# Value output products 1 to 3 from rounded parts, their rests and batch 1's right-operand sums on GpSimd

## What is computed

```python
Q = (img_embed @ Wq).reshape(B, -1, H, D).transpose(0, 2, 1, 3)
K = (sent_embed @ Wk).reshape(B, -1, H, D).transpose(0, 2, 1, 3)
V = (sent_embed @ Wv).reshape(B, -1, H, D).transpose(0, 2, 1, 3)
score = jnp.einsum('bhqd,bhkd->bhqk', Q, K) / math.sqrt(D)
attn = jax.nn.softmax(jnp.where(mask, score, -jnp.inf), axis=-1)
ctx = jnp.einsum('bhqk,bhkd->bqhd', attn, V).reshape(B, -1, H * D)
out = ctx @ Wo + img_embed
return (out - mu) * jax.lax.rsqrt(var + EPS) * gamma + beta
```

## Time and profile before

| | |
|---|---|
| median of 3 runs | 354.56 us (354.5 to 354.85) |
| the profiled execution | 354.68 us, of which 352.9 us are the span |
| TensorE | busy 347.1 us, 98% of the span |
| VectorE | busy 285.6 us, 81% |
| ScalarE | busy 238.8 us, 68% |
| GpSimd | busy 201.1 us, 57% |

### The profile page before, as it was taken

The page is one execution under the profiler, slowest core; times in us unless marked ns, Lnnn a source line. Parts: engine busy times, 40 slices in busy tenths (PEclk is TensorE's granted clock), DMA queues, the critical chain, the costliest instruction groups (busy, mean ns, idle before and its releaser), DMA issues.

```text
span 352.9 us, 6849 instructions
## 1 busy us (share of the span) xinstructions
PE 347.1 (98%) x2272; PEld 323.5 (92%) x2272; DVE 285.6 (81%) x523; ACT 238.8 (68%) x790; POOL 201.1 (57%) x212
## 2 busy tenths in 40 slices
PE   9999999999999999999999999999999999999994
PEld 6999999999999999998899899889988998899884
DVE  2159999999866467898798888987987989889896
ACT  3267766545555669887886976977778769768560
POOL 0045654400004858689769688688696796884243
PEclk9999999999999999999999999999999999999998
DMA  7999758775645070053142341440532423413012
GB/s 235 425 418 321 275 227 336 286 255 211 220 158 190 0 285 15 4 178 120 61 172 68 119 151 55 156 150 33 179 105 75 158 72 131 149 46 105 32 50 101
DMA packets 19683, 55.81 MB, mean 158 GB/s; under 512 B 1728, under 2 KB 3264, under 8 KB 17728
## 3 DMA queue, kind: packets, MB, share of 16 engines
q1 hardware_dynamic: 18784, 54.38, 42.2%
q10 hardware_dynamic: 864, 1.00, 1.1%
HBM read 46.98 MB, written 8.39 MB: 157 GB/s over the span
## 4 chain that ended last, share of the span: by engine, by line
PE 98%; DVE 0%; DVEq 0%; issue 0%
PE pair L670 30%; PE pair L595 27%; PE pair L480 17%; PE pair L487 15%; PE pair L657 5%; PE pair L585 1%; PE pair L692 1%; PE pair L687 1%; DVE centred L1187 0%; DVEq L103 0%; DVE stats_last L1179 0%; DVE mean_var L1184 0%; DVE var_eps L1159 0%; PE pair L605 0%; DVE out_sb L1173 0%
## 5 line engine op out<-in xcount | busy, mean ns | idle before, releaser
L670 PE MATMUL pair<-vw_hi,pt_hi 128*128 128x512 f32 x155 | 62.3, 402 | 0.0
L670 PE MATMUL pair<-vw_hi,pt_lo 128*128 128x512 f32 x155 | 60.9, 393 | 0.0
L670 PE MATMUL pair<-vw_lo,pt_hi 128*128 128x512 f32 x155 | 60.6, 391 | 0.0
L1312 POOL TENSOR_TENSOR out_sb<-centred,beta_sb 128x512 f32<-128x512 f32 x30 | 38.8, 1294 | 29.2 <-ACT centred L864 29.1
L1363 POOL TENSOR_TENSOR w_proj_lo<-w_proj,w_proj_hi 128x768 fp32r<-128x768 f32 x14 | 25.7, 1859 | 39.1 <-ACT w_proj_hi L755 39.1
L819 ACT ACTIVATE prob<-c,neg_max 128x77 f32<-128x77 f32 x128 | 43.9, 346 | 0.0
L480 PE MATMUL pair<-kv_t,w_out_hi 128*128 128x308 f32 x160 | 42.0, 336 | 0.0
L1357 POOL TENSOR_TENSOR xo_lo<-x_sum,xo_hi 128x512 fp32r<-128x512 f32 x32 | 41.4, 1299 | 0.5 <-ACT xo_hi L843 0.5
L595 PE MATMUL pair<-a_hi,xo_hi 128*128 128x308 f32 x128 | 40.4, 316 | 0.0
L1332 POOL TENSOR_TENSOR x_sum<-xt_in 128x256 f32<-128x256 f32 x16 | 11.9, 745 | 47.6 <-DMA xt_in<-x_tiles 47.4
L595 PE MATMUL pair<-a_hi,xo_lo 128*128 128x308 f32 x128 | 38.9, 304 | 0.0
(11 more groups left out here) (121 smaller groups left out, 1021.1 us busy)
## 6 DMA issues: line engine op xcount, KB each, us to landing
w_out<-wo SPq DMA_DIRECT2D x8, 1024.0 KB, 4.8
xt_in<-x_tiles SPq DMA_DIRECT2D x16, 512.0 KB, 4.0
x_in<-x_rows SPq DMA_DIRECT2D x16, 512.0 KB, 4.8
out<-out_sb SPq DMA_DIRECT2D x31, 256.0 KB, 2.2
w_out<-wq_t SPq DMA_DIRECT2D x7, 1024.0 KB, 7.6
w_proj<-wv SPq DMA_DIRECT2D x8, 768.0 KB, 4.7
w_proj<-wk SPq DMA_DIRECT2D x6, 768.0 KB, 9.6
w_out<-wq_t SPq DMA_DIRECT2D x2, 512.0 KB, 8.1
```

The costliest lines, as they stand in the source:

```text
L670: mm = pe.matmul(ps_out[:, i % 2, 0:s.model], ps[:, j, :], v[:, b, j, :], start=(j == 0 and n == 0), stop=(j == s.key_t - 1 and n == len(p ...
L1312: pool.tensor_tensor(out_sb[i % OUT_RING][:, :], centred[i % 2][:, :], beta_sb[:, :], ALU.add)\
```

## The change

Value products 9, 10 and 11 are split too. Their six half rests are divided: GpSimd makes those of uses 9 and 10 and the second half of 11, VectorE the first half of 11. GpSimd also makes the ten steps of batch 1's right sums; batch 0's stay on VectorE. T_PARTS is ordered by batch, so batch 1's sums are rounded and subtracted later, up to use 13. The sums' buffers no longer lie in the `xt_in` tiles themselves but in new tensors of other scopes over reused space, and `kv_full1`, the second whole value of the start, has one of its own. `add_kv`, which summed the two parts of use 9's values for a whole product, goes. The sequence of TensorE's matmuls changes in products 9 to 11 alone.

```diff
-    SPLIT_VALUES = (H, *range(H + 4, USES - 1))
+    SPLIT_VALUES = range(H, USES - 1)
+    POOL_HALVES = ((H + 1, 0), (H + 1, 1), (H + 2, 0), (H + 2, 1), (H + 3, 1))
...
-    T_PARTS = [(n, b) for n in (T1, T2, T4, T3) for b in range(s.batches)]
+    T_PARTS = [(n, b) for b in range(s.batches) for n in (T1, T2, T4, T3)]
...
@@ tensor
-                        pe.wait_ge(dve_o_lo, 2 * split_before(u) + half + 1)
+                        if (u, half) in POOL_HALVES:
+                            pe.wait_ge(pool_o_lo, rests_before(u, half, True) + 1)
+                        else:
+                            pe.wait_ge(dve_o_lo, rests_before(u, half, False) + 1)
...
@@ scalar, in the loop over u
                 if u == H + 1:
-                    for part in T_PARTS[:4]:
-                        round_t(*part)
+                    round_t(T1, 0)
                 elif u == H + 2:
-                    for part in T_PARTS[4:6]:
-                        round_t(*part)
+                    round_t(T4, 0)
                 elif u == H + 3:
+                    round_t(T3, 0)
+                    round_t(T1, 1)
+                elif u == H + 4:
+                    round_t(T4, 1)
+                elif u == H + 5:
                     round_t(T3, 1)
...
                 if u + 1 < USES and not whole_out(u + 1):
                     round_w_out(u + 1)
+                if u == H + 1:
+                    round_t(T2, 0)
+                elif u == H + 3:
+                    round_t(T2, 1)
                 take_out_product(u, 1)
...
@@ vector, in the loop over u
-                if u == H:
-                    right_sum(T1, 0)
...
+                if u == H + 1:
+                    split_t(T1, 0)
+                    right_sum(T4)
+                elif u == H + 2:
+                    split_t(T4, 0)
+                elif u == H + 3:
+                    split_t(T3, 0)
+                    split_t(T1, 1)
+                elif u == H + 4:
+                    split_t(T4, 1)
+                elif u == H + 5:
+                    split_t(T3, 1)
                 if not whole_out(u):
                     add_out_product(u, 0)
+                if u == H:
+                    right_sum(T1)
+                elif u == H + 1:
+                    split_t(T2, 0)
...
                 if not whole_out(u):
                     add_out_product(u, 1)
                 if u == H:
-                    right_sum(T1, 1)
-                    right_sum(T2, 0)
-                    right_sum(T2, 1)
+                    right_sum(T2)
                 elif u == H + 1:
...
+                    right_sum(T3)
...
@@ gpsimd
+            def split_w_out(u):
+                for half in range(2):
+                    if (u, half) in POOL_HALVES:
+                        pool.wait_ge(act_o_hi, 2 * split_before(u) + half + 1)
+                        pool.tensor_tensor(half_cols(w_out_lo[u % W_RING], half), half_cols(w_out_sb[u % W_RING], half),
+                                           half_cols(w_out_hi[u % 2], half).bitcast(F32), ALU.subtract)\
+                            .then_inc(pool_o_lo, 1)
...
+            split_w_out(H + 1)
+            split_w_out(H + 2)
+            right_sum(T1)
+            split_w_out(H + 3)
+            right_sum(T2)
+            right_sum(T4)
+            right_sum(T3)
             block_sums(0)
```

More of the change, by code:

```diff
@@ L157, in build @@
         with ExitStack() as spare:
-            t_tmp4 = [spare.enter_context(nc.sbuf_tensor(f"t_tmp4_{b}", [P, KT, s.half], F32)) for b in range(s.batches)]
+            kv_full1 = spare.enter_context(nc.sbuf_tensor("kv_full1", [P, s.dim_t, s.toks], F32))
         w_out_hi1 = sb("w_out_hi1", [P, s.model_t, s.dim_t, P], F32R)
@@ L163, in build @@
         vw_lo = sb("vw_lo", [P, s.batches, s.key_t, s.model], F32R)
+        with ExitStack() as spare:
+            t_tmp_x = [spare.enter_context(nc.sbuf_tensor(f"t_tmp_x{b}", [P, KT, s.half], F32)) for b in range(s.batches)]
+            t_tmp_z0 = spare.enter_context(nc.sbuf_tensor("t_tmp_z0", [P, KT, s.half], F32))
         xt_in = [sb(f"xt_in{n}", [P, CHUNK, s.model]) for n in range(XT_RING)]
@@ L171, in build @@
         t_lo0 = sb("t_lo0", [P, 3, KT, s.half], F32R)
+        with ExitStack() as spare:
+            spare.enter_context(nc.sbuf_tensor("gap7", [P, T4, KT, s.half], F32))
+            t_tmp_z1 = spare.enter_context(nc.sbuf_tensor("t_tmp_z1", [P, KT, s.half], F32))
         t_hi1 = sb("t_hi1", [P, 3, KT, s.half], F32R)
@@ L316, in whole_out, with rests_before @@
             return u < FULL_OUT or (u >= H and u not in SPLIT_VALUES)
-        def summed_kv(u):
-            return whole_out(u) and not whole(u)
         def split_before(u):
             return sum(not whole_out(v) for v in range(u))
+        def rests_before(u, half, by_pool):
+            return sum(((v, n) in POOL_HALVES) == by_pool for v in range(u + 1) if not whole_out(v)
+                       for n in range(2) if (v, n) < (u, half))
         def summed_before(u):
@@ L352, in use_w_proj, with t_in @@
             return use(u - (W_RING if u % W_RING < 2 else 0), W_RING)
[L354 to L360, removed]
+        t_tmp = [[t_tmp_x[0][:, :, :], prob1[:, :].rearrange("p (k n) -> p k n", k=KT), t_tmp_z0[:, :, :]],
+                 [t_tmp_x[1][:, :, :], t_tmp3[:, :, :], t_tmp_z1[:, :, :]]]
+        T3_IN = (2, 0)
+        def t_in(n, b):
+            return t_tmp[b][{T1: 0, T2: 1, T4: 0, T3: T3_IN[b]}[n]]
         def right_steps(b):
             x, y, z = t_tmp[b]
+            last = t_tmp[b][T3_IN[b]]
             hi = [[right(a_hi, b, half, cols).bitcast(F32) for cols in range(2)] for half in range(2)]
@@ L376, in steps_of, with t_done @@
             return range(T_STEPS[n - 1] if n else 0, T_STEPS[n])
-        def t_done(n, b):
-            ahead = [part for part in T_PARTS if t_no[part] <= t_no[n, b]]
-            return sum(len(steps_of(m)) for m, _ in ahead)
+        def t_done(n):
+            return T_STEPS[n]
         def batch_of(p):
@@ L491, in wait_kv @@
             def wait_kv(u, half):
-                if summed_kv(u):
-                    pe.wait_ge(dve_kv_sum, 2 * sum(summed_kv(v) for v in range(u)) + half + 1)
-                elif whole_out(u):
+                if whole_out(u):
                     pe.wait_ge(act_kv_hi, 2 * u + half + 1)
@@ L993, in split_kv @@
                        .then_inc(dve_kv_lo, 1)
[L995 to L1000, removed]
             def take_out_product(u, half):
@@ L1216, in _ @@
                     split_w_out(u + 1)
+                if u == H + 3:
+                    split_t(T2, 1)
                 if not whole_out(u):
@@ L1358, in split_sums, with right_sum @@
                                    xo_hi[p % 2][:, blocks, :, :].bitcast(F32), ALU.subtract).then_inc(pool_xo_lo, 1)
+            def split_w_out(u):
+                for half in range(2):
+                    if (u, half) in POOL_HALVES:
+                        pool.wait_ge(act_o_hi, 2 * split_before(u) + half + 1)
+                        pool.tensor_tensor(half_cols(w_out_lo[u % W_RING], half), half_cols(w_out_sb[u % W_RING], half),
+                                           half_cols(w_out_hi[u % 2], half).bitcast(F32), ALU.subtract)\
+                            .then_inc(pool_o_lo, 1)
+            def right_sum(n):
+                if n == T1:
+                    pool.wait_ge(dve_a_lo, 2 * H)
+                    pool.wait_ge(dve_kv_lo, 2 * split_before(FROM_FULL))
+                elif n in (T4, T3):
+                    before = (T1 if n == T4 else T4, 1)
+                    pool.wait_ge(act_t_hi, t_no[before])
+                    pool.wait_ge(dve_t_lo, t_no[before])
+                for k in steps_of(n):
+                    to, x, y, op = t_steps[1][k]
+                    if k:
+                        pool.wait_ge(pool_t, k)
+                    pool.tensor_tensor(to, x, y, op).then_inc(pool_t, 1)
             for u in range(FULL_PROJ, FROM_FULL):
```

48 lines of the change are left out of this document (16 added, 32 removed).

## The result

The changed kernel takes 366.74 us (366.7 to 366.88), the kernel before in the same rounds 354.56 us (354.5 to 354.91): ratio 1.0341 (1.0326 to 1.0356), 12.2 us slower. The forecast was 366.7 us. The profiled execution has a span of 365.1 us against 352.9, so the span holds the whole difference.

What follows compares the result with a forecast made beforehand. The prediction took TensorE's stream as the bound: 354.68 us profiled, plus 12.5 us of waits, less 0.5 us from shorter products, is +12.0 us, so 366.7 us; the 8 in 10 range was 361 to 371 us.

Steps and rivals of the forecast that it cites:

- part 1: Splitting shortens products 9, 10 and 11 on TensorE by 0.15 to 0.19 us each, together -0.5 us.
- The price of working at the same time: VectorE operations with two SBUF inputs and GpSimd's SBUF-reading ones block each other; without this the sum would be 354.2 us.
- The walk: Changed instructions laid engine by engine on the trace's times, with turns at the SBUF port; with the shorter products, +12.0 us.
- First wait: TensorE, halfway through product 9, waits for VectorE's addition for the second half of product 8: 1.0 us.
- Second: TensorE, after the projection of use 11, waits for VectorE's addition for the first half of product 9: 4.9 us.
- Third: TensorE waits for VectorE's kv_t operations of use 11, needed by the transposes inside product 10: 3.0 us.
- rival on the clock: A 4.9 us wait drops TensorE to the 1.2 GHz level, adding +2 to +4: 369 to 371 us; over 369: 0.11.
- Product 12: TensorE waits 0.7 us for VectorE's first rest and 1.5 us for the addition behind its second.
- Product 13: TensorE waits 0.4 us (119.8), as batch 1's sums on GpSimd meet VectorE's rests.
- Product 15: Late first-block load puts ScalarE's rounding ahead of its take-out of product 14; TensorE waits 0 to 2.3 us, 1.0 taken.
- As meant: The change shortens TensorE's stream without new waits, blocking belonging only to the earlier tiles: 354.2 us, chance 0.07.
- Slower by less: Two to three blocked turns in VectorE's queue before product 9's addition fall away: 359 to 363 us; 357 to 363.5: 0.14.

Runs made afterwards that it cites:

- `kv_t` first: The changed kernel with batch 0's three T3 steps moved behind the kv_t operations of use 11 on VectorE: 365.89 us, ratio 1.0320.

## Why the prediction was right

*What bounds the kernel, and part 1.* TensorE's stream was the time, and the one product without a wait gained as summed: product 11 with its projection takes 103.80 - 96.60 = 7.20 us, 7.35 before.

*GpSimd's operations.* The 616-column steps that met nobody took 1.50 to 1.53 us, 1.52 by the line through two rows. The rests come as 2370, 2622 and 2952 ns (least, median, most). The least is close to the 2.42 us forecast; the first of a pair took 2.62 and 2.37 us where 2.5 was named, the second 2.9 where 3.0 was.

*The price of working at the same time.* This was the step on which the forecast stood or fell, and it was read from two coincidences in the trace of before. The walk's 2.9 us for a step behind a rest came as 2.84 and 2.88. The turns came too: between 80.18 and 88.06 us the operations of VectorE and GpSimd end alternately, with VectorE's taking 2.50, 2.76 and 1.96 us. The fills show the cause: same places, same engine, no reads, and almost no price. The Trainium skill, SBUF — State Buffer, section Who interferes with whom, has VectorE's second SBUF input contending with GpSimd instructions that read SBUF, and not with those that only write it; the runs agree in both halves: 1.0345 with additions of two inputs, 0.9993 with fills.

*First wait*, 1.0 us: 1.04. *Second*, 4.9: 4.57, with the addition done at 88.45 against 88.7. *Third*, 3.0: 2.98 us are lost there, but the list shows 0.22. The walk had the right time for `kv_t` (94.55 against 94.8), and that set the time; TensorE, at half speed, was there only 0.22 us before it. Here the account was not complete. The clock fell, as the prediction's rival on the clock has it, and the slow matmuls filled the wait ("which that wait hides"). But the rival added +2 to +4 us for what would be left over, and no line of the forecast has a clock that falls and costs nothing more. It cost nothing more because it was back at 94.0, just ahead of `kv_t`. That is luck: behind the first long wait of the run with the rests on VectorE it stayed low for 6.6 us.

*Product 12*, 0.7 and 1.5 us: 0.90 and 1.18. *Product 13*, 0.4: 0.33. *Product 15*, 1.0: 0.31, or 0.5 by the shift. TensorE's waits there:

```profile
108.01 0.38 PE L489 MATMUL pair<-kv_t,w_out_hi 128*128 128x308 f32 x1 [0.90 <-DVE w_out_lo L986]
...
111.44 0.38 PE L489 MATMUL pair<-kv_t,w_out_hi 128*128 128x308 f32 x1 [1.18 <-DVE vw_t L1035]
...
120.06 0.38 PE L489 MATMUL pair<-kv_t,w_out_hi 128*128 128x308 f32 x1 [0.33 <-DVE vw_t L1035]
...
130.69 2.34 PE L496 MATMUL pair<-v_t,w_out 128*128 128x154 f32 x16 [0.31 <-DVE vw_t L1035]
```

The last term was too large. The block load was issued at 121.48 (122.0 forecast), its data were there by 126.0, 4.5 us later and near the lower of the two ends walked (4.0 and 6.3), and ScalarE got to its take-out of product 14 at 129.62. The path was the one walked: ScalarE's roundings of the first block stand ahead of this take-out, and the last of them waited 0.78 us for GpSimd's block sum, which had the data late. What made up for it is that a wait costs the stream more than its idle time in the list. The wait of 0.90 us moved the product from 103.80 + 3.05 = 106.85 to 108.01, 1.16 us; that of 1.18 us cost 1.34, the one of 1.04 about 1.2. Inside the stream a matmul of 0.34 us is followed by the next after 0.18; before a wait it runs to its end alone. Over six waits that is about 1 us that the sum had no term for. So the total, 366.7 against 366.74, is closer than its parts: errors of 0.2 to 0.7 us cancelled, and that is luck.

*The rivals.* As meant needed the blocking to belong to the tiles; 367.29 us with additions on foreign tiles rules that out. Slower by less needed a blocked turn of the second wait to fall away; none did, and the steps there end within 0.3 us of the walk.

## What to carry to other kernels

Before giving work to an idle engine, look for a moment in the trace where it already worked beside the busy one, and compare the length of the same instruction in and out of that moment: two such rows were worth more here than all busy shares. Where two-input SBUF operations of VectorE and GpSimd meet, count a turn for each meeting rather than each engine's own time, and follow the fixed row to the first instruction that TensorE needs. When a wait vanishes from the list, see by the granted clock and by starts, not by idle times, whether the time came back.

## What the runs showed of the hardware that was not expected

TensorE's clock fell in the middle of a kernel. The granted clock behind waits of 3.42 us (the run with the sums on VectorE), 4.1 (additions, twice), 4.56 (`kv_t` first), 4.57 (changed) and 4.68 us (rests on VectorE) went to the 1.2 GHz level; behind waits of 1.44 us and less it stayed at 1.00 in every trace. It does not seem to fall each time: of the four executions of the run with the sums on VectorE one has a mean clock of 0.999 where the others have 0.989, and it takes 364.51 us against 365.85 to 366.66; only one of the slower ones was traced. The Trainium skill, TensorE: Matmul & The Clock Gate, Part 1: The HAM clock gate, says that an idle TensorE falls back to the lower level, and the traces agree, with those waits. The way back was not the same each time: the matmuls were slow for 5.4 us after the wait in the changed kernel (to 94.0), for 4.3 with `kv_t` first (to 92.3) and for 6.6 with the rests on VectorE (80.53 to 87.16). In the last of these nearly all of product 9 ran slowly, 7.20 us up to the next projection against 4.15 for product 11 of the changed kernel. Why the way back differs, these runs don't show.

GpSimd's fills leave VectorE wholly alone (15.87 us of them, steps of 0.80 us), while its two-input operations on unrelated tiles make the same steps last 1.7 us. One operation of GpSimd and one of VectorE that meet come one after the other, whole: in the changed kernel GpSimd's second rest ends at 77.42 us and VectorE's step of 0.80 us at 78.08.
